# Routed feed-forward block on one core: each tile's weights and places read behind its rows, h2 split before it is turned

## The reference

```
h  = layernorm(x) * (1 + ca) + sa
a  = layernorm(h + sliding_attention(h, h, h, window 32))      # 16 heads of 8
a  = layernorm(a + relu(a @ W1 + b1) @ W2 + b2)
x  = x + ga * a
h2 = layernorm(x) * (1 + cb) + sb
scores = softmax(h2 @ gate_w.T)                                # 8 experts
w, idx = top_k(scores, 2)
out = sum over e of [w where idx == e] * ffn_e(h2)  +  ffn_shared(h2)
x = x + gb * out
```

## Time and profile before

| | |
|---|---|
| runs of the kernel before | 666.8, 654.73, 665.04 us; median 665.04 |
| the profiled execution, its own time | 664.14 us |
| its span, first to last instruction | 662.9 us |
| mean granted TensorE clock | 0.841 of full speed |
| busy: TensorE matmul, VectorE, ScalarE, GpSimd | 509.9, 473.0, 335.6, 422.9 us |
| attention part (first exp to last) | 57.5 to 341 us |
| rest of the units and shared expert | 341 to 480 us |
| loop over the tiles (first to last L579) | 483.9 to 622.2 us |

### The profile page before, as it was taken

How to read it: one execution, slowest core, us unless ns; L and a number is a source line. 1 busy time by engine, 2 the same in 40 slices (tenths; PEclk the granted TensorE clock), 3 DMA queues, 4 the chain that set the end, 5 groups by cost and what they waited for, 6 DMA issues and landing times.

```text
span 662.9 us, 17831 instructions
## 1 busy us (share of the span) xinstructions
PE 509.9 (77%) x6198; PEld 346.6 (52%) x6259; DVE 473.0 (71%) x1247; ACT 335.6 (51%) x786; POOL 422.9 (64%) x837
## 2 busy tenths in 40 slices
PE   2378998998979879898775669858755999899900
PEld 1134565565646546555453337535534888788700
DVE  2676876888689968774778687887643688788718
ACT  2104666776876656657663754647221444444300
POOL 4653546577787776867868794768703366566645
PEclk9755997998999969879696885869777999999955
DMA  6222322212120020000000000000312333443158
GB/s 168 81 72 72 98 66 77 87 52 81 35 67 2 13 79 11 19 11 18 19 11 24 18 25 9 19 17 25 105 26 52 72 79 62 99 80 80 38 145 235
DMA packets 69338, 38.88 MB, mean 59 GB/s; under 512 B 37871, under 2 KB 64629, under 8 KB 69252
## 3 DMA queue, kind: packets, MB, share of 16 engines
q1 hardware_dynamic: 64484, 29.25, 17.9%
q0 software_dynamic: 4544, 8.47, 4.0%
q10 hardware_dynamic: 224, 0.02, 0.0%
HBM read 18.59 MB, written 14.76 MB: 50 GB/s over the span
## 4 chain that ended last, share of the span: by engine, by line
PE 37%; DVE 15%; POOL 15%; SPq 12%; issue 8%; ACT 8%; DMA 4%; POOLq 0%; ACTq 0%; DVEq 0%
SPq L1251 4%; POOL scr_rows L1152 4%; PE ps L345 4%; PE ps L363 4%; PE ps L386 4%; PE ps L383 3%; SPq L1244 2%; SPq L1243 2%; ACT PT L645 2%; PE ps L409 2%; DVE H L782 2%; PE ps L402 2%; PE ps L426 2%; PE ps L342 2%; DVE rl L790 2%
## 5 line engine op out<-in xcount | busy, mean ns | idle before, releaser
L1233 POOL DMA_INDIRECT scr_back<-ysb,XM x78 | 79.1, 1014 | 77.5 <-DVE ysb L1053 62.6
L743 ACT ACTIVATE g<-ps,b1c 128x256 f32<-128x256 f32 x156 | 61.7, 475 | 93.3 <-PE ps L581 86.9
L645 ACT ACTIVATE PT<-ps 128x512 f32<-128x512 f32 x128 | 70.9, 596 | 22.2 <-PE ps L345 21.9
L1033 DVE TENSOR_REDUCE mx<-ps 128x4 f32<-128x384 f32 x128 | 67.3, 551 | 20.4 <-PE ps L386 20.1
L1152 POOL DMA_INDIRECT scr_rows<-PAY,SL x64 | 69.9, 1092 | 15.5 <-issue 15.3
L1044 DVE CAST gh<-g 128x512 f16<-128x512 f32 x78 | 34.6, 443 | 40.2 <-PE ps L597 35.6
L345 PE MATMUL ps<-QB,KS 97*128 97x256 f16 x256 | 55.5, 302 | 7.3 <-issue 5.5
L579 PE MATMUL ps<-xT,w1h 128*128 128x256 f16 x156 | 45.3, 290 | 17.1 <-DMA xT<-scr_rows 17.1
L594 PE MATMUL ps<-w2c,gh 128*128 x312 | 57.8, 223 | 0.7 <-DVE gl L1045 0.7
L1045 DVE TENSOR_TENSOR gl<-g,gh 128x512 f16<-128x512 f32 x78 | 55.6, 712 | 2.7
L595 PE MATMUL ps<-w2c,gh 128*128 x312 | 57.4, 221 | 0.0
(11 more groups left out here) (229 smaller groups left out, 1561.0 us busy)
## 6 DMA issues: line engine op xcount, KB each, us to landing
stg<-in_w_t SPq DMA_DIRECT2D x18, 256.0 KB, 2.9
KS<-scr_heads SPq DMA_DIRECT2D x24, 128.0 KB, 2.5
QS<-scr_heads SPq DMA_DIRECT2D x24, 128.0 KB, 2.9
X<-in_src SPq DMA_DIRECT2D x8, 256.0 KB, 5.0
H<-scr_back SPq DMA_DIRECT2D x8, 256.0 KB, 4.2
YB<-scr_back SPq DMA_DIRECT2D x8, 256.0 KB, 5.2
out<-X SPq DMA_DIRECT2D x8, 256.0 KB, 3.2
scr_back<-ysb,XM POOLq DMA_INDIRECT x78
```

The costliest lines, as they stand in the source:

```text
L645: A.activation(PT[:, k % 2, hf, :], ST[hf][:], ACT.Exp).then_inc(a_exp, 1)
L743: z = A.activation(g32[:, i % NG, TOKS * j:TOKS * j + TOKS], bank("first", i, half)[:, TOKS * jj:TOKS * jj + TOKS], ACT.Gelu, bias=b1f[:, ...
L1033: V.tensor_reduce(mx[:, n % 2, c, :], SM[c % 2][:, 0:384].rearrange("p (g k) -> p g k", g=4), AX.X, ALU.max).then_inc(v_max, 1)
L1233: G.indirect_dma_start(back_d, bass.IndirectOffsetOnAxis(ap=XM[:, i, c, 1:2], axis=0), ysb[:, i % NY, c, :], None, bounds_check=2 * NT * P ...
```

## The change

Three things are changed. The columns of a tile are loaded by fetch(i) itself, right behind its rows and with the same register, so that a value_load per tile goes; their semaphores are one per tile modulo NM = 12 instead of one per batch. H2_T now turns the payload: eight fp16 transposes of the high and low halves that PAY already holds, into one PSUM bank, which ScalarE copies into the unit's own part of H as fp16 (turned(u)); before them TensorE waits for p_tok, the end of GpSimd's payload subtraction. And the shared expert reads the same turned(u), so that SH_T and SH_LO with xsh and xsl are gone. In the steps, H2_T moves from 32 to 34 and GATE to DISPATCH each by one; for units 5 to 7 only H2_T (and for unit 7 GATE) moves, the rest of LATE stays.

```diff
-PAYLOAD, H2_T, H2_LO = steps(32, late="payload"), steps(32, late="h2_T"), steps(34, late="h2_lo")
-GATE, ROUTE_A, ROUTE_X = steps(34, late="gate"), steps(35, late="route_a"), steps(36, late="route_x")
...
+PAYLOAD, H2_T = steps(32, late="payload"), steps(34, late="h2_T")
+GATE, ROUTE_A, ROUTE_X = steps(35, late="gate"), steps(36, late="route_a"), steps(37, late="route_x")
+ROUTE_B, ROUTE_P, ROUTE_C = steps(38, late="route_b"), steps(39, late="route_p"), steps(40, late="route_c")
+DISPATCH = [steps(41 + t, late="dispatch", later=t) for t in (0, 1, 2, 4)]
...
+        def turned(u):
+
+            return unit(H, u).rearrange("p t d -> p (t d)").bitcast(F16).rearrange("p (h n) -> p h n", h=2)
...
                 for u in H2_T.get(k, ()):
-                    if norm_on_scalar(u):
-                        T.wait_ge(p_shifted[3], u + 1)
-                    else:
-                        T.wait_ge(v_shifted[3], u - NU + 3)
-                    transposed("h2T", u, unit(H, u))
+                    bk = take("h2T", u).bitcast(F16)
+                    T.wait_ge(p_tok, u + 1)
+                    for n in range(8):
+                        t = T.transpose(bk[:, 128 * n:128 * n + 128],
+                                        PAY[:, u % 2, n % 4, 0].bitcast(F16)[:, D * (n // 4):D * (n // 4) + D], id16[:])
+                    fill(t, "h2T", u)
...
                 for u in H2_T.get(k, ()):
-                    if u:
-                        A.wait_ge(*full("gate", u - 1))
-                    high("h2T", u, xh[:, 1, :])
-                for u in SH_T.get(k, ()):
-                    if u >= 2:
-                        A.wait_ge(*full("sh1", u - 2, 3))
-                    high("sT", u, xsh[:, u % 2, :])
+                    A.wait_ge(*full("h2T", u))
+                    A.activation(turned(u).rearrange("p h n -> p (h n)"), bank("h2T", u)[:].bitcast(F16),
+                                 ACT.Copy).then_inc(frees("h2T", u), 1)
...
-                for u in H2_LO.get(k, ()):
-                    low("h2T", u, xh[:, 1, :], xl[:, 1, :])
...
-                    V.wait_ge(d_xm[i // 8], 16 * min(8, NTL - i // 8 * 8))
+                    V.wait_ge(d_xm[i % NM], 16 * (i // NM + 1))
...
-            def columns_of(i):
-
-                r = Y.value_load(RWI[0:1, i:i + 1], min_val=0, max_val=8 * CAP)
-                Y.dma_start(XM[:, i], rows_d[bass.ds(r, TOKS), D:D + 2].rearrange("(c p) w -> p c w", p=P)).then_inc(
-                    d_xm[i // 8], 16)
-
             def fetch(i):
...
                 Y.dma_start_transpose(xT[:, i % NR], rows_d[bass.ds(r, TOKS), 0:D].bitcast(F16)).then_inc(d_xt[i % NR], 16)
+                Y.dma_start(XM[:, i], rows_d[bass.ds(r, TOKS), D:D + 2].rearrange("(c p) w -> p c w", p=P)).then_inc(
+                    d_xm[i % NM], 16)
...
                 fetch(i)
-                if i == 2 or i % 8 == 4:
-                    for n in range((i + 4) // 8 * 8, min((i + 4) // 8 * 8 + 8, NTL)):
-                        columns_of(n)
```

More of the change, by code:

```diff
@@ L64 @@
 LN4_A, LN4_N, LN4_B = steps(27, late="ln4_a"), steps(29, late="ln4_n"), steps(30, late="ln4_b")
-PAYLOAD, H2_T, H2_LO = steps(32, late="payload"), steps(32, late="h2_T"), steps(34, late="h2_lo")
-GATE, ROUTE_A, ROUTE_X = steps(34, late="gate"), steps(35, late="route_a"), steps(36, late="route_x")
-ROUTE_B, ROUTE_P, ROUTE_C = steps(37, late="route_b"), steps(38, late="route_p"), steps(39, late="route_c")
-DISPATCH = [steps(40 + t, late="dispatch", later=t) for t in (0, 1, 2, 4)]
+PAYLOAD, H2_T = steps(32, late="payload"), steps(34, late="h2_T")
+GATE, ROUTE_A, ROUTE_X = steps(35, late="gate"), steps(36, late="route_a"), steps(37, late="route_x")
+ROUTE_B, ROUTE_P, ROUTE_C = steps(38, late="route_b"), steps(39, late="route_p"), steps(40, late="route_c")
+DISPATCH = [steps(41 + t, late="dispatch", later=t) for t in (0, 1, 2, 4)]
 ATT_A, ATT_B = steps(3, 2, NT), steps(4, 2, NT)
@@ L71 @@
 MODULATE, GATES = steps(-14, 1, B - 1), steps(3, 16, B)
-SH_T, SH_LO, SH_1, SH_1B, SH_R, SH_RB, SH_2, SH_OUT = (steps(k, 3) for k in (67, 69, 70, 71, 71, 72, 74, 76))
+SH_1, SH_1B, SH_R, SH_RB, SH_2, SH_OUT = (steps(k, 3) for k in (70, 71, 71, 72, 74, 76))
 def adaln_block_kernel(nc, src, c_t, wmod, ln1_g, ln1_b, ln2_g, ln2_b, aw1, ab1, aw2, ab2,
@@ L135, in adaln_block_kernel @@
         onesb = sb("onesb", [P, P], BF16)
-        xh = sb("xh", [P, 2, F], F16)
-        xl = sb("xl", [P, 2, F], F16)
+        xh = sb("xh", [P, F], F16)
+        xl = sb("xl", [P, F], F16)
         r32 = sb("r32", [P, 2, F])
@@ L222, in adaln_block_kernel @@
         d_xt = [sem(f"d_xt{i}") for i in range(NR)]
-        d_xm = [sem(f"d_xm{w}") for w in range(NW)]
+        d_xm = [sem(f"d_xm{i}") for i in range(NM)]
         d_y = [sem(f"d_y{i}") for i in range(NY)]
@@ L459, in tensor_program @@
                         cs = slice(128 * t, 128 * t + 128)
-                        T.matmul(o, xh[:, 1, cs], gth[:], start=True, stop=False)
-                        T.matmul(o, xh[:, 1, cs], gtl[:], start=False, stop=False)
-                        t = T.matmul(o, xl[:, 1, cs], gth[:], start=False, stop=True)
+                        T.matmul(o, turned(u)[:, 0, cs], gth[:], start=True, stop=False)
+                        T.matmul(o, turned(u)[:, 0, cs], gtl[:], start=False, stop=False)
+                        t = T.matmul(o, turned(u)[:, 1, cs], gth[:], start=False, stop=True)
                     fill(t, "gate", u)
@@ L526, in tensor_program @@
                                   start=False, stop=True, skip_group_check=True), "rank", u)
-                for u in SH_T.get(k, ()):
-                    if norm_on_scalar(u):
-                        T.wait_ge(p_shifted[3], u + 1)
-                    else:
-                        T.wait_ge(v_shifted[3], u - NU + 3)
-                    transposed("sT", u, unit(H, u))
                 for u in SH_1.get(k, ()):
@@ L684, in scalar_program @@
                         A.wait_ge(*full("ff1", u - 1, 3))
-                    high("x1T", u, xh[:, 0, :])
+                    high("x1T", u, xh[:])
                 for u in FF_1.get(k, ()):
@@ L871, in vector_program @@
                         frees("att", t), 1)
-                for u in SH_LO.get(k, ()):
-                    low("sT", u, xsh[:, u % 2, :], xsl[:, u % 2, :])
                 for u in SH_R.get(k, ()):
```

27 lines of the change are left out of this document (12 added, 15 removed).

## The result

| | before | after |
|---|---|---|
| runs on the same chip | 666.8, 654.73, 665.04, 658.15 us; median 661.6 | 666.6, 668.26, 664.9, 665.31 us; median 665.95 |
| ratio after to before | | 1.015, 95% interval 1.008 to 1.022 |
| profiled execution, its span | 664.14, 662.9 us | 666.6, 665.1 us |
| mean granted TensorE clock | 0.841 | 0.833 |
| busy: TensorE, VectorE, ScalarE, GpSimd | 509.9, 473.0, 335.6, 422.9 us | 507.8, 462.3, 333.7, 420.9 us |

The changed kernel does less work on each engine and is no faster: 1.5% slower by this measurement, with an interval that reaches just past the 2% counted as no change, so it can't be told from no change.

A forecast was written before the change was run, and what follows sets the result against it. TensorE and SyncE's late issues were taken to bound the kernel after 484 us, TensorE and VectorE taking turns in attention before. 664.1 - 17.0 + 2 - 3 = 646.1, say 646 us, range 634 to 658.

The forecast's parts named there:

- The tiles, -17.0: Tile loop: TensorE's idle time and the slower matmuls after it go with columns behind rows; -17.0 us, bounds -17.5 and -13.
- Rival C: Tile loop: row loads cannot overlap columns ahead of them, 3.97 us a tile, 676 us in all; chance 0.03.
- the row: Tile loop: profile row where tile 3's rows, issued behind eight column loads, are used 3.01 us later; fetches stay at 3 us.
- Attention, +2: Steps 0 to 64: -1.45 + 0.7 + 1.3 = +0.55 us per unit, +2 us for four; bounds -8 and +14.
- ROUTE_B without cover: Attention, VectorE: ROUTE_B's 3.3 us now stand behind the wait for L554, ROUTE_C returns 1.4; +1.3 us per unit.
- The gain of the vanished L554 stall and subtraction: Attention: TensorE's wait of L554 for L786 and VectorE's 0.68 us subtraction go; 1.45 us gained per unit, units 0 to 3.
- The wait on ROUTE_A's copy: Attention: L554 waits for the bank that ROUTE_A's first copy frees; +1.2 us on TensorE, taken as 0.7 per unit.
- Behind attention, -3: Steps 65 to 97: GpSimd's payloads start earlier, TensorE's new payload wait falls into slack; -3 us, bounds -10 and +5.
- rival D: Behind attention: TensorE waits for GpSimd's payload, 10 us each in units 5 and 7; 667 us, slower; chance 0.06.
- A: Attention: uncovered ROUTE_B and the wait on ROUTE_A give back +12 us, later part gains nothing; 659 us; chance 0.17.
- B: Attention and behind it both gain: four stalls worth 2 us each, GpSimd's 6.16 us comes through; 634 us; chance 0.12.
- The forecast's own test: Whole kernel: the forecast is wrong if the time lies above 652 us, which the tiles alone can't explain.

The follow-up runs named there:

- e1_tiles: The kernel before with the columns part alone (columns loaded behind their rows, 12 semaphores), h2 turned as before; 645.48 us, ratio 0.984.
- e5_routeb: e3_steps with ROUTE_B, ROUTE_P, ROUTE_C and DISPATCH of units 0 to 4 one step later; 664.59 us, ratio 1.017.
- e3_steps: The changed kernel with H2_T at step 33 and GATE to DISPATCH at their old steps for units 0 to 4; 645.39 us, ratio 0.981.
- e7_before_shift: e1_tiles, h2 turned as before, with only GATE to DISPATCH of units 0 to 4 one step later; 666.72 us, ratio 1.021.
- e13_late5: e8_late7 with H2_T and GATE of unit 5 also one step later; 668.5 us, ratio 0.971.
- e14_beside: e1_tiles timed again, on the same chip as e13_late5; 672.48 us, ratio 0.981.
- e11_h7: e3_steps with unit 7 alone turned from H in fp32 as before, without the wait for the payload; ratio 0.979.
- e8_late7: e3_steps with H2_T, GATE, ROUTE_A, ROUTE_X and ROUTE_B of unit 7 one step later; 637.6 us, ratio 0.976.

## Why the prediction was wrong, point by point

The forecast was 646 us within 634 to 658; measured were 665.95. Against the profiled execution before, the sum said -18.0 and the spans say +2.2.

**The tiles, -17.0: right.** -16.7 in the changed kernel, -17.1 by the spans in e1_tiles. The idle time that goes, 3.18 us a tile and the 2.6 us pace of SyncE came as said, only 19 us later in the execution; the 0.4 us for a late tile at the start came twice, at tiles 1 and 4. Rival C, loads of rows held up by the columns ahead of them, is excluded: it wanted 3.97 us a tile. So the row decided rightly against reading the ring order rule of the Trainium skill's page DMA: Bandwidth & Descriptors as a delay: with the columns of another tile ahead of every load of rows but the first, no tile from 5 on was late.

**Attention, +2: wrong, the measured value is +10.0.** Its mechanisms were the right ones; the step that failed is the size of one term. "ROUTE_B without cover" was taken at +1.3 per unit, with an upper bound of 3.3 + 0.9 = 4.2. Measured alone, by e5_routeb against e3_steps, ROUTE_B and what follows it one step later cost 17.7 us in this stretch, 6.9, 4.1 and 5.1 us in units 0, 1 and 2, so 5.4 per unit and above the bound; e7_before_shift against e1_tiles gives 16.9 us. VectorE's wait itself grew as forecast, to 3.96 us in units 0 to 2, and that alone spoke against the term: from 0.9 to 4 us is 3 us more a unit. What I took as an excuse for the low value, that VectorE might be the later engine anyway, was answered by the trace of before. In units 0 to 3 it idled 0, 0.91, 2.40 and 1.25 us at this very place; of these has only the one of 0.91, and the two larger ones are, on VectorE's timeline before,

```profile
300.77 0.26 DVE L866 RECIPROCAL rden<-ps 128x16 f32<-128x16 f32 x1 [2.40 <-PE ps L554]
...
337.31 0.26 DVE L866 RECIPROCAL rden<-ps 128x16 f32<-128x16 f32 x1 [1.25 <-PE ps L554]
```

In three units of four TensorE was the later one there, and taking work out from ahead of the wait only lengthened it. In unit 0 VectorE came 0.7 us after TensorE's transposes (216.82 against 215.71 + 0.44), less than the 3.3 us that were moved, and the shift cost most. I also left out who is queued behind ROUTE_B: the row maxima, and behind them TensorE (4.85 us), whose granted clock fell behind the stall. ROUTE_B at its new place takes up to 4.7 us, not 3.3, since it runs beside GpSimd there, but that is not what made the loss (last section). The gain of the vanished L554 stall and subtraction I put at 1.45 us per unit; it came out at 6.3 us in four on one chip (e13_late5 against e14_beside) and at 9 to 10 us on two others, so 1.6 to 2.5 per unit. The wait on ROUTE_A's copy, 0.7 per unit, was about right.

**Behind attention, -3: wrong, the measured value is +9.7.** The step that failed is the charge for TensorE's waits for the payload, which the term puts "into slack of about that size" and counts in unit 5 alone. I had priced the one in unit 5, as 6 us into slack, and that about holds (at most 2.4 us by e11_h7). Unit 7's was not in the term at all, only in rival D. It was 13.10 us in e3_steps and cost 6.0 (e11_h7). The expected gains did not come: unit 5's payload was to end near 385 and ended at 402.87 (400.75 + 2.12), where only 9.3 us of the delay came out of attention, and the later dispatch of unit 4 was no help but part of the shift, which costs 4.7 us here (e7_before_shift 146.7 against 142.0). GpSimd's 6.16 us of idle time ahead of unit 6's payload did shrink, to 0.97, as the prediction's sign had it. But it was no price of the old way of turning h2: e1_tiles, which keeps that way, has 0.14 us there in one execution and 6.14 in another (e14_beside).

**The rivals.** What happened is A and D together, to which I had given at most 0.03: A in attention, where its +12 for the uncovered ROUTE_B and the bank was close to the +10 measured, and D behind it, with its waits of 10 us each in units 5 and 7 (6.81 us and the longest one, 14.2 us, in the trace). D's 667 us were nearest to the result, and that by luck: only half of its 20 us lay on the path, and A's loss in attention made up for the rest. B and C are out. The forecast's own test, a time above 652 that the tiles alone can't explain, has fired.

**The small terms.** Eight fp16 transposes took 0.61 us at a granted clock of 1.00 (e8_late7, units 0 to 2; 0.6 taken) and 1.01 us at 0.50, as in all of units 4 to 7 of the changed kernel; the copy of 128x1024 on ScalarE took 1.02 us (1.05 taken). TensorE's wait for ROUTE_A's copy was 4.5 us in four units (1.2 each taken at the most).

## What to carry to other kernels

- A wait on an engine is also a hiding place for what stands ahead of it. Before moving instructions past a wait, read on that engine's timeline, for every unit, whether it idles there at all, even for 0.9 us: then the moved work costs its full length or more, since what is queued behind it comes later too. No idle time is no safety either: in unit 0 VectorE came 0.7 us after the awaited result, and moving 3.3 us of work still cost 6.9 us there. Compare the lead with the length of what is moved.
- When a stage starts to read another engine's result (here TensorE the payload of GpSimd), list that wait for every unit, above all the last ones, and put the other work of the waiting engine ahead of it. One step in a table made the stretch 4.5 us shorter.
- The best kernels measured are the changed one with its steps put back and unit 7's transposes behind the shared expert's matmuls, e8_late7 (637.6 us, ratio 0.976), and the same with unit 5's one step later, e13_late5 (ratio 0.971 on its chip); their intervals overlap, and both lie below those of the two kernels compared here. How much of this is due to the h2 part is less sure, since the columns' part alone has 0.984 and 0.981 (e1_tiles, e14_beside), with overlapping intervals. Two changes in one diff hid each other; run apart, one gained 17 us and the other lost a little more.
